# Leaving out 34 unread bf16 products of TensorE ahead of the router's class counts

## What is computed

```python
xn2 = layer_norm(xn, ln_g, ln_b)                      # attention
q, k, v = split(xn2 @ qkv_w + qkv_b)
k = k * sigmoid(xn2 @ gate_w + gate_b)
q, k = elu(q) + 1, elu(k) + 1
num = (tril(q @ k.T)) @ v;  den = sum(q * cumsum(k)) + 1e-6
attn = num / den

scores = (xn @ router_w.T + router_b) / temperature   # experts
gates = sinkhorn(scores, 3)                           # 8 experts
vals, idx = top_k(gates, 2)
all_out = (relu(xn @ wg[e]) * (xn @ wp[e])) @ wo[e]   # 256 hidden
ffn = xn + sum(all_out[idx] * vals / sum(vals))
```

## Time and profile before

| what | us |
|---|---|
| median of 3 runs | 360.12 |
| lowest and highest | 357.38, 361.24 |
| the profiled execution's own time | 358.37 |
| its span, first to last instruction | 356.6 |

### The profile page before, as it was taken

How to read it: one execution, slowest core, us unless ns; L and a number is a source line. 1 busy time by engine, 2 the same in 40 slices (tenths; PEclk the granted TensorE clock), 3 DMA queues, 4 the chain that set the end, 5 groups by cost and what they waited for, 6 DMA issues and landing times.

```text
span 356.6 us, 8758 instructions
## 1 busy us (share of the span) xinstructions
PE 325.1 (91%) x2560; PEld 299.5 (84%) x2560; DVE 266.7 (75%) x726; ACT 236.2 (66%) x437; POOL 266.7 (75%) x364
## 2 busy tenths in 40 slices
PE   0799979878999999997999999999999999999991
PEld 0688748655888888886999999999989999999991
DVE  3998889999989888887667676667666766667661
ACT  2679853433767767666777775778667777777640
POOL 3596999975777776657577777777777777777776
PEclk9999999999999999999999999999999999999998
DMA  6999999999544342358599987617665566574110
GB/s 169 289 292 336 333 334 303 283 301 268 178 151 150 117 139 98 125 144 241 158 318 367 357 255 221 171 40 195 190 193 160 147 169 166 144 220 128 47 49 16
DMA packets 64189, 70.97 MB, mean 199 GB/s; under 512 B 6002, under 2 KB 59006, under 8 KB 64144
## 3 DMA queue, kind: packets, MB, share of 16 engines
q1 hardware_dynamic: 54016, 48.70, 50.3%
q0 software_dynamic: 8672, 21.19, 16.4%
q10 hardware_dynamic: 1456, 0.53, 0.6%
HBM read 28.54 MB, written 43.04 MB: 201 GB/s over the span
## 4 chain that ended last, share of the span: by engine, by line
PE 73%; DVE 16%; issue 3%; POOL 2%; DMA 2%; ACT 2%; SPq 0%; ACTq 0%; DVEq 0%
PE psum L1795 17%; PE psum L1780 9%; PE psum L1782 8%; PE psum L1781 8%; PE psum L1659 4%; PE psum L1677 4%; PE psum L1463 3%; PE psum L1595 3%; PE psum L1770 2%; POOL out L614 2%; DVE stats L910 2%; DMA rows<-in_L_attn_x 2%; PE psum L1516 2%; PE psum L1518 2%; PE psum L1520 2%
## 5 line engine op out<-in xcount | busy, mean ns | idle before, releaser
L614 POOL DMA_INDIRECT out<-rows x70 | 68.9, 984 | 21.3 <-issue 17.1
L592 POOL DMA_INDIRECT by_lower<-rows,slot_u x64 | 62.6, 978 | 26.8 <-issue 17.5
L1780 PE MATMUL psum<-xT_high,w_now 128*128 128x256 f32 x256 | 77.0, 301 | 1.9 <-DVE xT_low L1387 1.1
L825 ACT ACTIVATE w_now<-w_split 128x1024 fp32r x63 | 66.7, 1059 | 14.8 <-PE psum L1782 14.8
L1795 PE MATMUL psum<-w_expert,hT 128*128 x560 | 75.4, 276 | 1.0 <-DVE hT L1396 0.7
L1781 PE MATMUL psum<-xT_low,w_now 128*128 128x256 f32 x256 | 71.6, 280 | 0.0
L1782 PE MATMUL psum<-xT_high,w_now 128*128 128x256 f32 x256 | 71.5, 279 | 0.0
L603 POOL DMA_INDIRECT by_upper<-rows x58 | 57.2, 987 | 18.0 <-issue 10.6
L1400 DVE TENSOR_TENSOR hT<-relu,psum 128x512 f32<-128x512 f32 x64 | 44.0, 687 | 35.6 <-ACT relu L844 19.4
L1795 PEld LDWEIGHTS psum<-w_expert,hT 128*128 128x128 f32 x560 | 68.7, 191 | 1.4 <-issue 1.3
L844 ACT ACTIVATE relu<-psum 128x512 f32<-128x512 f32 x64 | 38.2, 598 | 22.0 <-PE psum L1782 21.6
(11 more groups left out here) (277 smaller groups left out, 665.5 us busy)
## 6 DMA issues: line engine op xcount, KB each, us to landing
by_lower<-blank SPq DMA_DIRECT2D x1, 10140.0 KB, 34.7
by_upper<-blank SPq DMA_DIRECT2D x1, 10062.0 KB, 73.3
rows<-by_upper SPq DMA_DIRECT2D x32, 258.0 KB, 2.9
rows<-by_lower SPq DMA_DIRECT2D x26, 260.0 KB, 4.5
rows<-in_L_attn_x SPq DMA_DIRECT2D x8, 512.0 KB, 9.5
lead_row<-by_lower SPq DMA_DIRECT2D x6, 260.0 KB, 4.1
out<-rows POOLq DMA_INDIRECT x70, 2.8
w_expert<-in_L_ffn_wg SPq DMA_DIRECT2D x8, 128.0 KB, 3.0
```

Of the source, the lines that this page charges most:

```text
L592: pool.indirect_dma_start(by_lower, bass.IndirectOffsetOnAxis(ap=slot_u[:, t:t + 1], axis=0), rows[:, t, :], None)\
L614: pool.indirect_dma_start(out_rows, bass.IndirectOffsetOnAxis(ap=row(n)[:, k, TOKEN:TOKEN + 1].bitcast(U32), axis=0), row(n)[:, k, BASE], ...
L825: act.activation(w_now[:, n % 2, :], w_split[:, bass.ds(number, 1), 0:4 * FF].rearrange("p a f -> p (a f)"), ACT.Copy).then_inc(w_copied, 1)
L1780: pe.matmul(target, high, x_high, start=True, stop=False)
```

## The change

The 34 products in TensorE's stream are left out. Nothing takes their place.

```diff
             add_state(2, 0)
             add_state(2, 1)
             add_state(2, 2)
-            for _ in range(34):
-                pe.matmul(psum[:, ROUTE_BANK, 0:P], before_h[:], before_h[:], start=True, stop=True)
             route_counts()
             route_totals()
             project(3, "q")
```

## The result

The changed kernel takes 360.92 us in the median of 19 runs (359.33 to 364.41), the kernel before 359.09 us in 19 runs on the same chips (357.38 to 361.24). The ratio is 1.0055, with a 95% interval from 1.0035 to 1.0074: slower by half a percent, inside the 1% that I had called no change. The profiled execution took 359.42 us, with a span of 357.7.

A forecast was written before the change was run, and what follows sets the result against it. It took VectorE's chain of small router operations, not TensorE, to bound the changed place. Profiled 358.37 us + 0 (hidden products) + 1.3 (clock fall) = 359.7, or 361.4 us from the runs' median 360.12; range 358.4 to 364.2.

The forecast's parts named there:

- The products were hidden: Ahead of the counts: removing 34 products takes off 2.06 us, 0 on the path, since counts wait for `member` until 76.00.
- The clock falls: From 73.75 to 77.58 TensorE does next to nothing for 3.83 us; a fall to half clock was somewhat more likely.
- the two cases with a fall: Around q of group 3: clock falls and returns as at the start (0.48, 361.4 us), or stays low longer (0.13, 364.0).
- the two ends of the trace: At the kernel's end 3.85 us without work lowered the clock; the 1.71 us wait before 84.94 did not.
- The price: At `placed`: q and places at half clock make it 1.0 to 2.3 us late; 1.3 us was taken.
- low when q starts at 77.58, high again about 81.8: From q of group 3: half clock lasts 4.2 us, carried over from the clock's rise at the kernel's start.
- its bounds of 0.47 and 1.77: Products of the places, 78.55 to 80.32: half clock adds at least 0.47 us, at most 1.77.
- the 0.35 us of slack: Before `placed`: places end at 80.39, VectorE arrives at 80.74, so 0.35 us comes off the delay.
- "Hidden" behind the 1.71 us wait: Behind the places: TensorE's 2.9 us of work, 1.4 to 1.7 us late, ends before 85.3, ahead of `kp` at 86.2.
- The second rival: From q to group 3's scores: the low clock lasts, TensorE holds up the scores, +3.9 us, 364.0 us; chance 0.13.
- Through to the end "in full": From group 3's scores at 84.94 to the end: the 1.3 us delay carries through whole.
- The faster case: At the counts: 34 products delay some executions; removal gains at most 2.06 us, estimated half a microsecond, 359.6 us; chance 0.05.

The follow-up runs named there:

- run 9: The changed kernel (34 products left out) once more, on the same chip as a filled kernel: 360.86 us in 12 runs, ratio 1.0033 to the kernel before.
- Run 1: Kernel before with its 34 products moving one column each instead of 128: ratio 1.0045 to the kernel before.
- run 2: Kernel before with 17 of its 34 products kept: ratio 1.0031 to the kernel before.
- runs 5 and 6: Kernel before plus 28 products ahead of group 3's scores, ratio 1.0022; kernel before plus 40, 5, 4 and 9 products before TensorE's first real work, ratio 1.0007.

## Why the prediction was right, and where not

- **The products were hidden: right.** The counts wait 2.20 us for `member` and start when it is written. Nothing was won by taking 2.06 us of work off TensorE.
- **The clock falls: right,** and more surely than I had said: at this place in both profiles of the changed kernel, and somewhere in the middle of at least 29 of its 31 executions (those of the result and of run 9), where the two cases with a fall had a chance of 0.61 together. The argument from the two ends of the trace was the useful one: the stretch with hardly any work counts, not its longest gap alone. Run 1 shows it for products of one column, run 2 for gaps no longer than one that did no harm in the earlier trace rows. What I had not seen is that the stretch isn't safe with the 34 products either (runs 5 and 6). The rule of the Trainium skill (TensorE: Matmul & The Clock Gate, section "Why this matters for your kernels") would have had no fall, as no gap reaches 3 us; the longest here is 2.20 us, so where page and runs differ the runs decide.
- **The price: mis-sized, 2.20 us in the profile against 1.3,** though inside the 1.0 to 2.3 that I had given for it. The step that failed is "low when q starts at 77.58, high again about 81.8". The clock was low from 75.4 on, before the counts, and up again at 85.6: 10.2 us instead of 4.2. Term by term, from the earlier trace rows to the rows after: counts to q 1.58 to 1.89 us, +0.31, where I had nothing (the 14 counts take 0.91 instead of 0.60 us); q 0.97 to 1.87, +0.90, as forecast; places 1.77 to 2.93, +1.16, inside its bounds of 0.47 and 1.77, where I had leaned to the low end. These less the 0.35 us of slack make 2.02, and `placed` is 2.06 us late, not 1.3. So the path was the one forecast, over `placed` and `kp`, and two of its terms were too small.
- **"Hidden" behind the 1.71 us wait: wrong, in this profile by 0.1 us.** The state product, the outputs and the gate product took 4.45 instead of 2.91 us, +1.54, where I had almost nothing. TensorE's four terms together are 3.91 us; less the wait of 1.71 us that took them up, 2.20. That is 0.11 us more than VectorE's chain is late. In run 9's profile of the same kernel TensorE decides plainly: `kp` is written at 86.84, the scores start at 87.76, 11.59 us after the counts, so the fall cost 2.65 us there:

```profile
76.17 0.60 PE L1620 MATMUL psum<-ones_h,member 128*64 128x1 bf16 x14 [2.20 <-DVE member L1109]
...
87.76 1.05 PE L1659 MATMUL psum<-qp,kp 128*128 128x128 f32 x8
```

- **The second rival's mechanism,** that TensorE itself is what the scores wait for, is what happened behind the places, by little here and by 0.9 us in run 9. I had priced it at 3.9 us for a clock low throughout all that work and with the wait already taken off. Its sum took 5.8 us for the last part (4.45 measured: up to the gate product the rows grew from 1.89 to 3.59 us, nearly double, but the gate product itself ran at the full clock) and 1.77 for the places (1.16).
- **Why not back after 4.2 us, as at the start?** That stays open. At the start TensorE ran fp32 products of 128 and 136 columns one upon the other. Here the places stand in the low stretch, and at half clock their L1638 and L1641 products are still spaced 0.48 us. I suspect these small products; that was not tried by itself. In run 9 the clock fell only at 77.4, just before q, and was low for 10.2 us too; in runs 2, 5 and 6, where it fell during q or the places, it was back after 6.8 us (at 84.9, 85.5 and 85.8).
- **Through to the end "in full": nearly.** The delay is 1.43 us at group 15's scores (163.27 against 161.84), where 2.20 less the 0.63 us of the faster start would be 1.57. TensorE's last product is 1.39 us later (350.69 against 349.30), the span 1.1 us longer (357.7 against 356.6). At the very end both profiles have GpSimd's scatters 1.29 us apart without a wait for TensorE, the last of them at 353.98 and 355.03; that took up the rest.
- **The size in the medians** is 1.83 us. The kernel before isn't free of falls itself; on run 9's chip its 7 executions that kept the clock have 358.56 us and the changed kernel's median is 2.3 us above that. A low mean clock doesn't always cost time, though: of before's 31 in the first comparison, seven with a mean of 0.983 took 358.45 to 358.89 us, no more than those that kept it (358.52). Which falls these were no profile shows.
- **The number: partly luck.** 361.4 forecast, 360.92 measured. The base, a median of 3 runs, was 360.12 where 19 runs gave 359.09, so 1.03 us too high, and the added 1.3 us was 0.53 less than the 1.83 that the medians show. The second error hides half of the first.
- **The faster case** found nothing: no execution of the changed kernel is under 359.3 us.

## What to carry to other kernels

Work that nobody reads can still earn its place by keeping TensorE's clock up, and it costs nothing as long as it ends before the wait it fills. Before taking such products out, price what runs behind them at half clock, until the clock is really back: here the places grew by a factor of 1.66 and the fp32 products by 1.9, and a wait behind them hides only its own length. Look at the mean clock of many executions, not of one profile: one profile of before showed a clean row, while about half of its executions lost the clock somewhere. Such products change how often the clock falls, not whether it can.

## What the runs showed that I had not expected

The longest gap alone doesn't decide a fall: with 17 products and gaps of at most 1.71 us in this stretch 9 of 10 executions lost the clock, while before, with gaps just as long, keeps it in 36 of 84. What the products change is how often it is lost. Counted by mean clocks, so without the place: no products 29 of 31; 34 of one column 10 of 10; 17 products 9 of 10; 34 products 46 of 84; 68 products 1 of 10; all four waits filled 0 of 22.

A warm start (2.09 instead of 3.96 us for the first logits) was worth nothing (1.0007): the path there runs over VectorE's rows, for which TensorE then waits at 24 us, and the clock falls in that wait. And the same place falls at different times in different executions of one kernel: at 75.4 and 77.4 us in two profiles of the changed one, 0.0 and 1.2 us after the counts began.
